# A scan of 64 steps in a six-layer perceiver block: the loop of four turns is written out on three engines

## What is computed

```python
def step(carry, inp):
    ln, nm, sg = carry
    a_t, b_t, vl_t, vs_t = inp
    ln = _stable_lse(a_t + ln, b_t)
    dec = a_t[..., None] + nm
    new = b_t[..., None] + vl_t[:, None, :]
    m = jnp.maximum(dec, new)
    ssum = sg * jnp.exp(dec - m) + vs_t[:, None, :] * jnp.exp(new - m)
    nsg = jnp.sign(ssum)
    nm = m + jnp.log(jnp.abs(ssum) + EPS)
    y = (nsg * jnp.exp(nm - ln[..., None])).sum(-2)
    return ((ln, nm, nsg), y)
_, ys = jax.lax.scan(step, (ln0, nm0, sg0), xs)
```

## Time and profile before

| | |
|---|---|
| Time before, median of 3 runs | 2352.98 us (2350.37 to 2353.34) |
| The profiled execution, its own time | 2354.67 us |
| Its span in the trace | 2352.8 us |
| First L1617 of the scan to the last L1633 of it | 1860.49 to 2049.07 us |
| TensorE, VectorE, ScalarE busy over the whole span | 89%, 46%, 40% |

### The profile page before, as it was taken

One profiled execution on the slowest core, in us unless ns is written; L12 is line 12 of the kernel. 1 busy time (PEld: TensorE's weight loads), 2 busy tenths in 40 slices (PEclk: granted clock), 3 DMA queues, 4 the chain that ended last, 5 costly groups with the idle time before them and its releaser, 6 DMA issues. The chain is left out here.

```text
span 2352.8 us, 30151 instructions
## 1 busy us (share of the span) xinstructions
PE 2090.8 (89%) x9904; PEld 1469.2 (62%) x9904; DVE 1084.6 (46%) x2172; ACT 930.5 (40%) x1699; POOL 123.4 (5%) x138
## 2 busy tenths in 40 slices
PE   7979962999999759999999999999979499877999
PEld 5647862555555348787878777787757377633443
DVE  4655552010100135444352626343355599839992
ACT  5743320111111034445454545444344477615550
POOL 0000013000000110000000000000000000002220
PEclk9989875999999979999999999999989555588999
DMA  7410024777778421010000001010021700000000
GB/s 258 132 38 1 0 103 174 306 290 311 310 289 319 173 85 41 15 52 27 27 27 27 27 27 40 13 40 27 1 90 45 252 1 1 1 5 0 1 14 23
DMA packets 35591, 212.41 MB, mean 90 GB/s; under 512 B 5059, under 2 KB 5060, under 8 KB 27974
## 3 DMA queue, kind: packets, MB, share of 16 engines
q1 hardware_dynamic: 32966, 203.28, 22.9%
q0 software_dynamic: 2560, 8.39, 1.1%
HBM read 189.04 MB, written 22.61 MB: 90 GB/s over the span
## 5 line engine op out<-in xcount | busy, mean ns | idle before, releaser
L106 PE MATMUL PS<-cT,qs 128*128 128x512 f32 x1152 | 293.5, 400 | 7.0 <-ACT pb L1203 7.0
L106 PE MATMUL PS<-pT,cN 128*128 128x512 f32 x1152 | 270.3, 392 | 1.7 <-DVE pT L1299 1.7
L106 PEld LDWEIGHTS PS<-cT,qs 128*128 128x128 f32 x1152 | 208.4, 188 | 57.1 <-issue 15.1
L901 PE MATMUL PS<-W,xgT 128*128 128x384 f32 x736 | 242.8, 488 | 1.4 <-ACT xgT L924 1.4
L106 PEld LDWEIGHTS PS<-pT,cN 128*128 128x128 f32 x1152 | 213.9, 188 | 45.5 <-DVE pT L1299 1.9
L901 PEld LDWEIGHTS PS<-W,xgT 128*128 128x128 f32 x736 | 140.4, 191 | 104.2 <-issue 11.3
L1198 ACT ACTIVATE qp<-PS 128x512 f32<-128x512 f32 x192 | 110.9, 596 | 196.8 <-PE PS L106 189.8
L106 PE MATMUL PS<-ws,xT 128*128 128x512 f32 x672 | 170.2, 412 | 11.4 <-DVE ws L1510 6.3
L1294 DVE TENSOR_REDUCE nmax<-PS 128x1 f32<-128x512 f32 x128 | 87.7, 685 | 160.5 <-PE PS L106 160.4
L106 PEld LDWEIGHTS PS<-ws,xT 128*128 128x128 f32 x672 | 131.9, 200 | 46.8 <-issue 18.0
L952 DVE TENSOR_TENSOR hid<-gated,PS 128x384 f32<-128x384 f32 x46 | 23.4, 551 | 277.5 <-PE PS L877 235.6
(11 more groups left out here) (225 smaller groups left out, 3161.1 us busy)
## 6 DMA issues: line engine op xcount, KB each, us to landing
W<-in_fc SPq DMA_DIRECT2D x23, 3072.0 KB, 12.6
W<-in_proj SPq DMA_DIRECT2D x23, 1536.0 KB, 6.7
cT<-in_ctxT SPq DMA_DIRECT2D x16, 768.0 KB, 5.7
ct_in<-in_ctxT SPq DMA_DIRECT2D x16, 768.0 KB, 4.3
cn_in<-in_ctxN SPq DMA_DIRECT2D x16, 768.0 KB, 5.0
W<-in_w SPq DMA_DIRECT2D x2, 4096.0 KB, 24.5
routed_x<-zero SPq DMA_DIRECT2D x23, 256.0 KB, 5.4
xg<-routed_x SPq DMA_DIRECT2D x23, 256.0 KB, 5.8
```

Source lines behind the costliest of these rows:

```text
L106: mm = nc.tensor.matmul(out, lhs(m, s), rhs(n, s), start=(opens and (s, m, n) == terms[0]), stop=((s, m, n) == terms[-1]))
L901: mm = nc.tensor.matmul(ps[c][:, 0:HFE], xgT[:, k, :], fc[u][:, k, c * HFE:(c + 1) * HFE], start=(k == 0), stop=(k == DK - 1))
```

## The change

The three loops become Python loops, so that the builder writes all 64 steps into each engine's program. Nothing else differs: the same operations on the same tiles in the same order, and the same semaphores. In the built program VectorE has 332 instructions in the loop (one turn, with those that wait or set registers), run four times, and 1031 instructions for the same work afterwards; ScalarE's program grows from 1159 to 1300 instructions, TensorE's from 4697 to 5027 (a product counted as two, its weight load and itself).

```diff
@@ VectorE
-                with ve.Fori(0, S // (2 * G)) as i:
+                for i in range(S // (2 * G)):
                     for j in range(2 * G):
                         t = 2 * G * i + j
@@ ScalarE
                 turn(0, True)
-                with act.Fori(0, S // (2 * G) - 1) as i:
+                for i in range(S // (2 * G) - 1):
                     turn(i + 1, False)
@@ TensorE
                 for j in range(AHEAD):
                     values(0, j)
-                with pe.Fori(0, S // (2 * G) - 1) as i:
+                for i in range(S // (2 * G) - 1):
                     turn(i, False)
                 turn(S // (2 * G) - 1, True)
```

## The result

| | before | changed |
|---|---|---|
| Median, 7 runs each | 2352.57 us (2348.99 to 2353.34) | 2344.53 us (2341.21 to 2345.42) |
| Ratio to before | | 0.9969, 95% interval 0.9958 to 0.9981 |
| The profiled execution: time, span | 2354.67, 2352.8 us | 2341.21, 2339.4 us |
| Scan, first L1617 to first half of the last L1617 | 1860.49 to 2046.18: 185.69 us | 1855.62 to 2032.47: 176.85 us |

The median fell by 8.0 us; 8.1 was forecast. A second set of five executions of the changed kernel, beside its own runs of before, gave 2341.61 us and a ratio of 0.9959 (0.9945 to 0.9972).

What follows compares the result with a forecast made beforehand. VectorE's chain of 64 scan steps was taken to bound the kernel; removing three jump holes gave -8.1 us, all other terms 0, so the median goes from 2352.98 to 2344.9 us, range 2341.3 to 2349.0.

Steps and rivals of the forecast that it cites:

- What bounds: In the scan, VectorE's chain of 64 steps, 2.805 us each, with three holes, sets the time.
- The three holes: At VectorE's three turn ends in the scan, jumps back leave idle time; removing them gives -8.1 us.
- What makes the jump cost: VectorE's long loop body, counted as 332 instructions, makes each jump back stall 2.7 us; shorter bodies on other engines do not.
- The other rule weighed: At 108 ns per compare-and-branch, VectorE's three branches would be worth 0.3 us, so no change.
- TensorE and ScalarE: 0: Their jumps in the scan, 0.1 to 0.3 us each, lie in idle time that VectorE ends; worth nothing.
- Register work: 0, and 60 ns for a column of numbers stay: Removing register operations between VectorE's steps gains 0; L1617's extra 60 ns come from reading a column and stay.
- The small delays: In each VectorE turn's eighth and fifteenth step, 0.23 us a turn; change taken as 0, bounds -0.9 to +0.9.
- The copy of a full bank: ScalarE's copy in a turn's second step, 1.05 us more, is absorbed by the two `bv` buffers; worth 0.
- The clock behind the scan: TensorE's clock rises after the scan may shift relative to the work: up to 2.5 us either way, most likely nothing.
- Straight code does not stall: Rival claimed the opposite: written-out VectorE code stalls at six stops, +7.8 us, 2360.8 us; chance 6%, milder form 4%.
- A hole that isn't the jump's: Rival: something else at VectorE's turn heads costs 2.7 us and stays; no change, 2353 us; chance 3%.
- A larger gain by constants in place of registers: Rival: scan steps start their waits sooner, 0.05 us a step, 3 us more gain, 2341.7 us; chance 4%.

Runs made afterwards that it cites:

- the variants without padding: Padding: already met waits added behind every step of the kernel with VectorE turns of eight steps, until a turn has 330 instructions; 2483.78 us.

## Why the prediction was right

- **What bounds.** Right. VectorE's chain sets the scan; its pace of 2.80 to 2.81 us a step is the same in every one of the variants without padding, and what was won there came through to the end.
- **The three holes, 8.07 us.** Right in size and in place: the holes of VectorE's jumps are gone, and undoing the change on VectorE alone brings them back (2353.47 us).
- **What makes the jump cost.** Here the step failed, though the sum didn't need it. "What differs is the length of the body" is refuted by the loops shifted by 40 and 80: the same length, no holes. (The counts ahead were also slightly off, since they took in what stands around the loop: the body has 322 instructions, not 332, and written out the scan has about 1020.) A body of 322 fails on four blocks and passes on three. The transfer that no row of the prediction showed is in the trace, 1.0 us behind each branch. The rule of the Trainium skill (Runtime: NRT & Kernel Launch, Instruction fetch mechanics) has the right mechanism, a taken jump out of what is held. But its block of 256 instructions with two held doesn't fit VectorE or ScalarE here: the packets of that queue hold 8.2 KB, on VectorE they and the short delays come 128 instructions apart, and with edges only every 256 the loops at 700 to 1022 and at 816 to 1138 could not both have been one block too long while those at 740 and 780 were not. The other rule weighed, the 108 ns of the Trainium skill (Advanced Engine Details and Errata, Control Flow Timing) for a compare-and-branch, lies between the 50 to 63 ns of the branch alone in VectorE's scan and the 0.14 to 0.25 us (0.53 once) that a jump costs here when it doesn't miss. Of a jump that misses that section says nothing.
- **TensorE and ScalarE: 0.** Right; the run with those two alone moved nothing.
- **Register work: 0, and 60 ns for a column of numbers stay.** Right for the pace, which stayed 2.80 us, and for the 60 ns: L1617 has a median of 515 ns after the change, L1633 of 455. But 515 was expected near 482; all durations grew, as told below.
- **The small delays: I took 0, with a bound of -0.9.** Mis-sized. Of 185.69 us, 63 steps of 2.805 are 176.72, the holes 8.07, and 0.90 is left; of 176.85 after only 0.13. So 0.8 us of them went. I had supposed that written-out code meets as many edges and is delayed at them. It meets some eight, about 1020 instructions in blocks of 128, and shows no delay at any but for its longer first step. Why a loop pays 0.03 to 0.13 us at an edge and straight code nothing isn't settled; that it has fewer instructions a step, 16 against 20, and its sequencer so keeps further ahead, would explain it, but wasn't tried.
- **The copy of a full bank: 0.** Right: no step behind a seam is longer.
- **The clock behind the scan: 0, up to 2.5 either way.** Right: the stretch behind the scan took 303.7 and 304.0 us.
- **The rivals.** Straight code does not stall: about 1020 instructions in a row, the first of them while the weight loads keep the DMA engines full (share 1.05 at 1860 to 1864), without a hole. A hole that isn't the jump's but comes of the register work at a turn's head is out by the loops shifted by 40 and 80, which do the same register work there and have none. A larger gain by constants in place of registers is out too: the pace is the same with either.

The forecast was right for a reason that was half right. Had the loop stood 40 instructions later in the program, the same reading of its length would have promised 8 us from a change that could give 0.6 (its scan takes 177.45 us, the changed one 176.85). The evidence that carried the sum was the silent sequencer behind the branch, not the count of instructions.

## What to carry to other kernels

Look behind the branch of each hardware loop on the engine that sets the pace: a few tenths of a microsecond to the sequencer's next instruction is a loop that costs almost nothing, 2.4 to 3.0 us is a miss, paid at every jump back. A view of the DMA queues for that silence has one packet of code in it where the jump missed, 1.0 to 1.2 us behind the branch. The cure is to write out that engine's loop alone, to shorten the turn, or to move the loop so that it touches fewer blocks; and since the place decides, an edit ahead of the loop can bring the misses or take them away. By the theory of blocks that holds for bodies of some 260 to 380 instructions on VectorE and ScalarE, which touch three blocks or four as they lie; longer ones always touch four. The bounds are an estimate: only bodies of 162, 322 and 327 were moved. A comparison of two kernels that differs by a few microseconds a loop may show nothing else.

## What was not expected of the hardware

Jumps of VectorE and ScalarE miss when the loop touches four blocks of 128 instructions, not at a length: 322 instructions cost 0.14 to 0.18 us a jump at two places and 2.6 to 2.8 us at two others, with 5 packets of 8.2 KB more for each miss. TensorE showed no miss at all; its loop in the cross attention (L1186), which leaves 1349 records a turn in the trace (a product leaves two), has its next register operation 0.3 us after the branch.

When the loops of all three engines are written out, the recorded durations of VectorE's operations grow while their pace does not. L1633 of the changed kernel (ns, min/median/max):

```profile
L1633 DVE TENSOR_TENSOR W1s<-W1s x128: 420/455/471, 1858.0 to 2034.9; 128x256 f32<-128x256 f32 x128
```

With VectorE's loop alone written out the same line has a median of 415, with the other two alone 416, and in the kernel before 422; the second set of the changed kernel has 437. Its halves start 0.335 us apart in all of them, so the records overlap more and the longer ones cost nothing; whoever adds up busy time would read a slowdown that isn't there. What causes it wasn't tried.
